# Attention stage: the order of maxima pieces and scores in a step, the causal mask of the maxima, and the sum over experts

## What is computed

```
sx  = einsum('bsh,ndh->bnsd', x, hl_w) + hl_b
q   = einsum('bnsd,neod->bneso', sx, wq);  k = einsum('bnsd,nod->bnso', sx, wk);  v = ...
scores = einsum('bnesd,bntd->bnest', q, k) * d ** 0.5 + causal      # -inf above the diagonal
att = softmax(scores);  qkv = where(pad, 0, einsum('bnest,bntd->bnesd', att, v))
gs  = softmax(einsum('bnsf,nef->bnse', out, gate_w) + gate_b)
mixed = einsum('bnsed,bnse->bnsd', out, gs)                         # the sum over experts
hn  = layernorm(mixed + resid)
```

## Time and profile before

| | us |
|---|---|
| median of 3 runs | 3414.06 (3410.56 to 3416.23) |
| the profiled execution | 3411.35 |
| its span, first to last instruction | 3409.6 |
| PE busy over the span | 3022.5 (89%) |
| DVE busy | 1882.0 (55%) |
| ACT busy | 1284.8 (38%) |
| POOL busy | 1783.4 (52%) |
| line 1899, DVE's reads of maxima, 784 | 859.8 |
| line 1840, exponentials, 776 | 728.5 |
| line 1730, products of the pieces, 1568 | 341.8 |
| line 1735, their mask products, 832 | each 216 to 328 ns long, overlapping |

### The profile page before, as it was taken

One profiled execution on the slowest core, in us unless ns is written; L12 is line 12 of the kernel. 1 busy time (PEld: TensorE's weight loads), 2 busy tenths in 40 slices (PEclk: granted clock), 3 DMA queues, 4 the chain that ended last, 5 costly groups with the idle time before them and its releaser, 6 DMA issues. The chain is left out here.

```text
span 3409.6 us, 46365 instructions
## 1 busy us (share of the span) xinstructions
PE 3022.5 (89%) x18170; PEld 1857.4 (54%) x18170; DVE 1882.0 (55%) x2869; ACT 1284.8 (38%) x1712; POOL 1783.4 (52%) x957
## 2 busy tenths in 40 slices
PE   7998987589998899999999999789899999999953
PEld 3467656378875555555545555455555554545532
DVE  3545764477833456564565641255656465565566
ACT  2232320355533234334434344233343443434433
POOL 0030020332311366777888889546777878888014
PEclk9999888899998899999999999889999999999976
DMA  9961100399960000000000000000000000000001
GB/s 390 423 233 48 55 1 8 112 295 268 267 118 3 1 1 1 1 1 1 1 1 1 1 1 1 1 1 1 1 1 1 1 1 1 1 1 1 1 3 40
DMA packets 63607, 195.24 MB, mean 57 GB/s; under 512 B 8228, under 2 KB 24994, under 8 KB 53411
## 3 DMA queue, kind: packets, MB, share of 16 engines
q1 hardware_dynamic: 38642, 147.98, 11.3%
q0 software_dynamic: 24752, 44.31, 7.2%
HBM read 188.86 MB, written 3.41 MB: 56 GB/s over the span
## 5 line engine op out<-in xcount | busy, mean ns | idle before, releaser
L2029 POOL TENSOR_TENSOR at_acc<-at_acc,at_pt 128x1024 f32<-128x1024 f32 (+3 forms) x674 | 1455.1, 2159 | 271.5 <-ACT at_pt L1840 197.1
L1899 DVE TENSOR_REDUCE at_mx<-at_psR 128x2 f32<-128x1024 f32 (+3 forms) x784 | 859.8, 1112 | 812.4 <-PE at_psR L1730 527.7
L1840 ACT ACTIVATE at_pt<-at_psR 128x1024 f32<-128x1024 f32 (+3 forms) x776 | 728.5, 944 | 971.9 <-PE at_psR L1751 624.3
L1769 PE MATMUL at_psO<-at_pt,v 128*64 128x512 f32 (+3 forms) x3104 | 697.8, 571 | 9.8 <-DVE at_oT L1920 9.8
L1748 PE MATMUL at_psR<-at_qhi,at_klo 64*128 64x512 f32 (+2 forms) x1552 | 344.3, 439 | 68.2 <-DVE at_mx L1899 61.9
L1730 PE MATMUL at_psR<-at_khi,at_qhi 64*128 64x512 f32 (+3 forms) x1568 | 341.8, 430 | 38.8 <-DVE at_mx L1899 9.0
L1769 PEld LDWEIGHTS at_psO<-at_pt,v 128*64 128x64 f32 x3104 | 190.7, 137 | 326.6 <-issue 271.1
L1316 PE MATMUL ga_acc<-h,ga_ring 128*128 128x257 f32 (+1 forms) x1352 | 305.1, 386 | 30.1 <-ACT ga_ring L1210 26.6
L1748 PEld LDWEIGHTS at_psR<-at_qhi,at_klo 64*128 64x128 f32 x1552 | 149.8, 188 | 323.5 <-issue 304.4
L1316 PEld LDWEIGHTS ga_acc<-h,ga_ring 128*128 128x128 f32 (+1 forms) x1352 | 257.9, 193 | 75.6 <-ACT ga_ring L1210 34.7
L1748 PE MATMUL at_psR<-at_qlo,at_khi 64*128 64x512 f32 (+2 forms) x1552 | 298.8, 380 | 0.0
(11 more groups left out here) (331 smaller groups left out, 3442.3 us busy)
## 6 DMA issues: line engine op xcount, KB each, us to landing
gc_rows<-in_adj SPq DMA_DIRECT2D x26, 1664.0 KB, 17.4
ga_rows<-in_adj SPq DMA_DIRECT2D x26, 1664.0 KB, 10.0
ga_ring<-in_adjT POOLq DMA_DIRECT2D x78, 512.0 KB, 23.7
gc_cols<-in_adjT SPq DMA_DIRECT2D x26, 1024.0 KB, 14.9
gc_ring<-in_adjT SPq DMA_DIRECT2D x26, 512.0 KB, 8.0
gc_ring<-in_adjT SPq DMA_DIRECT2D x13, 256.0 KB, 2.8
ga_ring<-in_adjT POOLq DMA_DIRECT2D x13, 256.0 KB, 9.3
out_x<-X SPq DMA_DIRECT2D x6, 512.0 KB
```

The costliest lines, as they stand in the source:

```text
L1769: ins = pe.matmul(columns(psO[lanes[l], :], g), v1[:, t, (2 * hp + l) * D:(2 * hp + l + 1) * D], packed(pt[:, g % PTS, l, 0:w], g), start= ...
L1840: act.activation(pt[:, g % PTS, :, 0:w], psR[:, slot_of["score", g] % SLOTS, :, 0:w], ACT.Exp).then_inc(e_ready, 1)
L1899: dve.tensor_reduce(mx[:, u % 2, :, s, c:c + 1].rearrange("p l o -> p (l o)"), psR[:, slot_of["max", i] % SLOTS, :, 0:w], AX.X, ALU.max).t ...
L2029: pool.tensor_tensor(to, to, got, ALU.add).then_inc(added, 1)
```

## The change

In each step the order score, first piece, score, second piece (and third) becomes first piece, score, score, second piece (and third). The ring's order follows it. The causal mask of the diagonal pieces is no longer added by products: DVE reduces the columns left of the last 128 as before, and the last 128 with a fused add and maximum for each head (`tensor_tensor_reduce`, with `hide_row` now a float mask in SBUF), so a row can have one more partial maximum (`seen`). The four experts are added by one `tensor_reduce` over a view in which the expert is the innermost index, 512 bytes apart, into a new tile; the last block keeps the two additions. The query weights of the second head pair replace the first's in the same buffer by a later load. The core of the diff (declarations of semaphores, and numbers of waits that follow from it, are left out: PE and DVE wait for 8 of `hides` where PE waited for 9):

```diff
@@ slot_users @@
-            for half in range(2):
-                if g + 2 + half < FIRST[NU]:
-                    out.append(("score", g + 2 + half))
-                out += [("max", piece[0]) for piece in max_pieces(u, k, half)]
+            out += [("max", piece[0]) for piece in max_pieces(u, k, 0)]
+            out += [("score", x) for x in (g + 2, g + 3) if x < FIRST[NU]]
+            out += [("max", piece[0]) for piece in max_pieces(u, k, 1)]
@@ AttentionWeights @@
-        self.wq = m.sb("at_wq", [P, NPR, NE, P])
+        self.wq = m.sb("at_wq", [P, NE, P])
-        sp.dma_start(self.wq[:, :, :, :], io["wq2"].rearrange("n p e o -> p n e o")).then_inc(self.loaded, 16)
+        sp.dma_start(self.wq[:, :, :], io["wq2"][0]).then_inc(self.loaded, 16)
@@ stage_attention, tiles @@
-        hide_row = m.sb("at_hide_row", [P, 2, P], BF16)
+        hide_row = m.sb("at_hide_row", [P, P])
+        junk = m.sb("at_junk", [P, P])
-        mx = m.sb("at_mx", [P, 2, 2, SUB, NB + 1])
+        mx = m.sb("at_mx", [P, 2, 2, SUB, NB + 2])
+        mixed = m.sb("at_mixed", [P, SUB, P])
@@ SyncE @@
                 ffn.load(sp, io)
+                for hp in range(1, NPR):
+                    sp.wait_ge(x_full, turn_of["q", FIRST_UNIT[hp] - 1] + 1)
+                    sp.dma_start(wq_sb[:, :, :], io["wq2"][hp]).then_inc(wq_loaded, 16)
@@ TensorE, queries @@
+                    if hp and u == FIRST_UNIT[hp]:
+                        pe.wait_ge(wq_loaded, 16 * hp)
@@ TensorE, row_max @@
-                    diag = c == (c0 // P + s % (bw // P)) // SUB
                     for l in range(2):
                         ins = pe.matmul(psR[:, slot, l, 0:w], qhi[lanes[l], u % 3, s * P:(s + 1) * P],
-                                        khi[lanes[l], kc:kc + w], start=True, stop=not diag)
-                    if diag:
-                        for h in range(2):
-                            for l in range(2):
-                                ins = pe.matmul(psR[:, slot, l, w - P:w], isel[lanes[l], h, :], hide_row[lanes[l], h, :],
-                                                start=False, stop=h == 1)
+                                        khi[lanes[l], kc:kc + w], start=True, stop=True)
                     ins.then_inc(p1_full, 1)
@@ TensorE, main loop @@
-                        for half in range(2):
-                            if g + 2 < ng:
-                                scores(g + 2 + half)
-                            for piece in max_pieces(u, k, half):
-                                row_max(u + 2, *piece)
+                        for piece in max_pieces(u, k, 0):
+                            row_max(u + 2, *piece)
+                        if g + 2 < ng:
+                            scores(g + 2)
+                            scores(g + 3)
+                        for piece in max_pieces(u, k, 1):
+                            row_max(u + 2, *piece)
@@ VectorE, row_max @@
                     dve.wait_ge(p1_full, i + 1)
-                    dve.tensor_reduce(mx[:, u % 2, :, s, c:c + 1].rearrange("p l o -> p (l o)"),
-                                      psR[:, slot_of["max", i] % SLOTS, :, 0:w], AX.X, ALU.max).then_inc(p1_read, 1)
+                    if c < (c0 // P + s % (bw // P)) // SUB:
+                        dve.tensor_reduce(mx[:, u % 2, :, s, c:c + 1].rearrange("p l o -> p (l o)"), got[:, :, 0:w], AX.X,
+                                          ALU.max).then_inc(p1_read, 1)
+                        return
+                    if w > P:
+                        dve.tensor_reduce(mx[:, u % 2, :, s, c:c + 1].rearrange("p l o -> p (l o)"), got[:, :, 0:w - P], AX.X,
+                                          ALU.max)
+                    col = c + (w > P)
+                    if i:
+                        dve.wait_ge(p1_read, i)
+                    link(dve.tensor_tensor_reduce(junk[:, :], got[:, 0, w - P:w], hide_row[:, :], 1.0, -3.0e38, ALU.add,
+                                                  ALU.max, mx[:, u % 2, 0, s, col:col + 1]))
+                    dve.tensor_tensor_reduce(junk[:, :], got[:, 1, w - P:w], hide_row[:, :], 1.0, -3.0e38, ALU.add,
+                                             ALU.max, mx[:, u % 2, 1, s, col:col + 1]).then_inc(p1_read, 1)
@@ VectorE, maxima @@
-                        seen = (c0 // P + s % (bw // P)) // SUB + 1
+                        tile = c0 // P + s % (bw // P)
+                        seen = tile // SUB + 1 + (tile % SUB > 0)
@@ VectorE, gate, piece 2 @@
-                        link(dve.tensor_tensor(on[:, 0:ws, 0:2, :], on[:, 0:ws, 0:2, :], on[:, 0:ws, 2:4, :], ALU.add))
-                        link(dve.tensor_tensor(on[:, 0:ws, 0, :], on[:, 0:ws, 0, :], on[:, 0:ws, 1, :], ALU.add))
+                        if at_block < NPR * NQB - 1:
+                            link(dve.tensor_reduce(mixed[:, 0:ws, :], on[:, 0:ws, :, :].rearrange("p s e c -> p s c e"),
+                                                   AX.X, ALU.add))
+                        else:
+                            link(dve.tensor_tensor(on[:, 0:ws, 0:2, :], on[:, 0:ws, 0:2, :], on[:, 0:ws, 2:4, :], ALU.add))
+                            link(dve.tensor_tensor(mixed[:, 0:ws, :], on[:, 0:ws, 0, :], on[:, 0:ws, 1, :], ALU.add))
-                        dve.tensor_tensor(hsl, hsl, on[:, 0:ws, 0, :], ALU.add).then_inc(mix_done, 1)
+                        dve.tensor_tensor(hsl, hsl, mixed[:, 0:ws, :], ALU.add).then_inc(mix_done, 1)
@@ GpSimd, the mask @@
-                pool.memset(hide_row[:, :, :], 0.0).then_inc(hides, 1)
+                pool.memset(hide_row[:, :], 0.0).then_inc(hides, 1)
+                pool.affine_select(out=hide_row[:, :], in_=hide_row[:, :], compare_op=ALU.is_ge, fill=NEG, base=0,
+                                   pattern=[[-1, P]], channel_multiplier=1).then_inc(hides, 1)
+                pool.wait_ge(hides, 4)
                 for e in range(2):
-                    pool.affine_select(out=hide_row[lanes[e], :, :], in_=hide_row[lanes[e], :, :], compare_op=ALU.is_ge,
-                                       fill=NEG, base=0, pattern=[[D, 2], [-1, P]], channel_multiplier=1).then_inc(hides, 1)
```

More of the change, by code:

```diff
@@ L1450 @@
 UNITS = [(hp, b, e) for hp in range(NPR) for b in range(NQB) for e in range(0, NE, EXPERTS[b])]
+FIRST_UNIT = [[hp for hp, _, _ in UNITS].index(n) for n in range(NPR)]
 LAST_UNIT = {(hp, b): u for u, (hp, b, _) in enumerate(UNITS)}
@@ L1772, in values @@
                     ins.then_inc(pv_done, 1)
-                pe.wait_ge(hides, 9)
+                pe.wait_ge(hides, 8)
                 pe.wait_ge(consts, 3)
@@ L1872, in _ @@
                 dve.wait_ge(zeros, 1)
+                dve.wait_ge(hides, 8)
                 link = Linker(dve, chain)
@@ L1897, in row_max @@
                 def row_max(u, i, s, c, w):
+                    c0, bw = QBLOCKS[UNITS[u][1]]
+                    got = psR[:, slot_of["max", i] % SLOTS, :, :]
                     dve.wait_ge(p1_full, i + 1)
-                    dve.tensor_reduce(mx[:, u % 2, :, s, c:c + 1].rearrange("p l o -> p (l o)"),
-                                      psR[:, slot_of["max", i] % SLOTS, :, 0:w], AX.X, ALU.max).then_inc(p1_read, 1)
+                    if c < (c0 // P + s % (bw // P)) // SUB:
[12 more added lines that the diff above has]
+                                             ALU.max, mx[:, u % 2, 1, s, col:col + 1]).then_inc(p1_read, 1)
                 def maxima(u):
```

4 lines of the change are left out of this document (2 added, 2 removed).

## The result

The changed kernel takes 3363.18 us, median of 4 runs (3360.61 to 3364.28), beside 3412.31 us of the kernel before (3404.88 to 3416.23, 4 runs). The ratio is 0.9857, with a 95% interval from 0.9839 to 0.9876: 49 us faster. Forecast were 7 us, and the low end of the range, 3366 us, was too high by 3.

A forecast was written before the change was run, and what follows sets the result against it. PE was taken to set the pace in its program order, so its waits inside a step count. From 3411.35 us, -6 (order) + 29 - 8 - 4 (mask) - 4 (sum) = 7 gained: 3404 us; likeliest 3392 to 3412, 8 in 10 3366 to 3434.

The forecast's parts named there:

- order, plain two-piece steps: Plain steps with two pieces, 176: the second piece's wait of 0.23 us goes; 40 us gained.
- order, three pieces: Steps with three pieces, 60: the last piece still waits for the first score's exponential, 0.25 us; 5 us lost.
- order, first steps of units: First step of each unit, 48: second piece 0.69 us late behind DVE's work, before 0.23; 22 us lost.
- order, narrow steps: Steps with scores 256 and 128 wide, 44: second piece 0.44 us late in 36, before about 0.2; 9 us lost.
- order, behind gate pieces 0 and 2: Behind gate piece 0 the second piece is 1.3 us late, 10 lost; at gate piece 2 PE stops earlier, 26 lost.
- order, small blocks and unit ends: In small blocks and at unit ends the forecast booked no loss or gain for the order: 0.
- the sum, all gates: At gate piece 2, one reduction of 4.0 us replaces additions of 6.19, so DVE is free 2.2 us sooner; +22.
- the mask: In 208 diagonal pieces PE saves 0.14 us each, 29 gained; DVE's longer reads lose 8 and 4 where not hidden.
- PE's patience is shorter: At gate piece 2, PE gets through less work before stopping than in the old order; with the reduction, 4 us lost.
- rival 4: Products taken off PE stood in waiting time, order worth nothing on balance: 29 shrink to 12, 3421 at worst; chance 0.12.
- rival 3: At gate piece 2 the strided reduction is slower: from 5.7 us it turns the sum over, 7 us gives 3434; chance 0.10.
- Rival 1: New waits for DVE don't come, lateness being absorbed, or the reduction runs at 2.3 us: about 3365; chance 0.19.

The follow-up runs named there:

- The run with half an exponential: The kernel before, order untouched, with ScalarE's exponential over half the columns of each score, leaving out the other half: 3346.84 us, ratio 0.9811.
- near sum: The changed kernel with the reduction reading four neighbouring elements instead of four 512 B apart, leaving out the sum over experts: 3339.46 us, ratio 0.9791.
- mixed order: The changed kernel with the old order at each unit's first and last-but-one step and right behind gate pieces 0 and 2: 3312.73 us, ratio 0.9713.
- GpSimd's halves: The kernel before with GpSimd's running sum in two instructions of 512 elements in place of one of 1024: 3397.61 us, ratio 0.9966.
- near layout: The mixed order with the experts' results laid out so that the four of one sum are neighbours: 3308.96 us, ratio 0.9701.

## Why the prediction was wrong

The sum of the forecast can be cut anew, so that each of its terms has a measured partner: steps of that kind, in the run that has this part alone or, for the mask, added to order and sum. Gains are positive.

| term | forecast | measured |
|---|---|---|
| order, plain two-piece steps | +40 | +51 |
| order, three pieces | -5 | +7 |
| order, first steps of units | -22 | -18 |
| order, narrow steps | -9 | -4 |
| order, behind gate pieces 0 and 2 | -36 | -31 |
| order, small blocks and unit ends | 0 | -11 |
| the sum, all gates | +22 | +34 to +39 |
| the mask | +17 | +12 to +18 |

(The forecast's +40 counts 176 steps, the measured +51 the 148 of them outside the gates' steps. -36 is the -10 behind gate piece 0 and the 26 us by which "PE's patience is shorter" ate the reduction's 2.2 us in ten blocks and 4 more. +17 is 29 - 8 - 4.)

**What each step looks like, right.** The order does trade the wait for ACT against waits for DVE: 26 waits for the reads of maxima became 66 (some 100 were forecast), and they come where they were looked for. The narrow steps wait 0.24 ahead of the second piece, where 0.44 was forecast, and behind gate piece 0 the stall is 1.10 where 1.3 was. At a unit's start the loss has the size but not the place: not the second piece but the first waits, since a piece there waits for DVE's instruction on the queries' low half. The fused instructions cost what the earlier trace rows gave, the reduction 3.8 against 4.0. The mask's net 17 was right in the new order; taken alone it would have been wrong by all of it, since 76 of the pieces' masks stood in the exponential's shadow and DVE's longer reads took back what the others gave. That is rival 4's mechanism, and it holds in the old order only. In the new order, too, there is luck in the 17: by kinds of steps the mask gained 18 to 22 us and lost 6, where 29 and 12 were forecast, and the two misses cancel.

**Failed: the size of a removed wait** ("176 x 0.23 = 40 us gained"). The wait was read off as the gap in PE's starts. The start behind it, 0.43 in the earlier trace rows between piece and values, was taken for a piece's price; 0.10 of it came from the wait. Over the 148 plain steps that are not at gates, 0.345 us each is 51, where 0.23 would be 34; the other 28 of the forecast's 176 stand in the measured row of the gates.

**Failed: the three-piece steps** ("The old stall survives ... 5 lost"). The last piece's wait was seen in the new order, and the old order was given one wait too, for the exponential. The run with half an exponential shows that the old one was for DVE. One stall took the place of another that was longer: 12 us between forecast and run.

**Failed: the length of DVE's absence** ("So DVE is free 2.2 us sooner"). The reduction alone is 2.4 us shorter than the additions that it replaces, about the 2.2 forecast. But 10.76 less 2.2 was taken to leave the 2.71 of the `hn` addition as it stood in the earlier trace rows. That row is no price; the plain price of 512 elements is 0.69, and the rest was waiting for GpSimd. The additions had each been paying it. Absence was 7.22, 1.4 us shorter than forecast, in each large block, 11 us over eight of them. In the old order the clock comes on top, 0.8 us a block on average, which no term had.

The Trainium skill, SBUF — State Buffer, section Who interferes with whom, calls the port pair of VectorE and GpSimd an exclusive lock, in which whoever issues first holds it for the whole instruction. The prediction drew on that section for the reduction, and left out what follows for the addition behind it. The ends at +0.55 agree with it. By its rule the three instructions that read two SBUF operands pay for what is left of a GpSimd instruction, and only one such instruction is left after the change.

The Trainium skill, SBUF — State Buffer, section Door 1: The DMA port swizzle, says that each access that crosses to a new line of 16 bytes pays a penalty, so that by it both strides pay alike. The trace agrees: 0.74 ns an element at 512 bytes and 0.8 at 32, so the upper end of 5.5 us was not needed.

The first two failures are 23 us, the third 11, the smaller losses at gates, narrow steps and first steps some 14; the small blocks, a loss of 11 that no term had, go the other way. That leaves some 5 us of the 42 between 7 and 49 without a name: the parts' sums over steps hold 45 of the 49.

**Two slips in the working**, neither of which moved the forecast. A read of 512 elements costs 0.69 us by the earlier trace rows, not 0.65, so the masked first piece would have been read by 2.17 and not 2.13, still inside 2.18. And rival 3's "from 5.7 us on it turns the sum over" doesn't follow from its own price: at 10 us for each us of the reduction, 7 us gained are used up at 4.7.

**The range.** Rival 1 had the time, about 3365, but not the reason: the losses that it left out did come, and that its number fits is luck. The range's lower end rested on losses absorbed and not on a removed wait being dearer than its gap.

## What to carry to other kernels

Price a removed wait by comparing the same stretch of code with and without it elsewhere in the trace, the restart included, not by the gap alone. Before a part is called worthless, ask what else hides it: the mask's products cost nothing until the wait beside them was gone, so parts that are nothing alone may be worth doing together. A new order need not hold everywhere: kept for plain steps and undone at unit starts, narrow steps and behind gate pieces it gave 99 us instead of 49. And once the longest stall is short, look for the engine that it had hidden: here GpSimd's additions.

## What the runs showed of the hardware

- A `tensor_tensor` on DVE with both operands in SBUF that starts while a GpSimd addition runs ends at a fixed distance behind that addition's end: 0.55 us for 512 elements, 1.08 for 1024, 0.28 for 256, 0.15 for a 128-element product, whatever the GpSimd instruction's length (0.7 to 3.2 us). Of 512, 1024 and 128 elements they take 0.69, 1.22 and 0.29 us alone. Even 32 elements took 1.88 us so (0.19 alone). GpSimd's additions that start while such an instruction runs are longer too, 3.15 and 2.60 us in unit 22 where their mean is 2.39. A `tensor_reduce` of 2048 neighbouring elements took 2.27 to 2.29 us, beside a running addition or not.
- A reduction over fp32 elements 512 bytes apart takes 3.79 us for 2048 elements, over neighbours 2.29. ScalarE's copy of 256 elements takes 384 ns written densely and 642 written 16 bytes apart.
- Behind a wait of some 0.2 us PE needs 0.10 us more until the values' first products than it does in an unbroken row.
- How long PE stood still does not by itself tell its granted clock afterwards. Over the six blocks with gate piece 2: behind 5.84 to 6.18 us (before, changed kernel) it was 1.2 GHz at once in all; behind 3.48 to 3.78 (near sum) at once in four and within a microsecond in two; behind 2.51 to 2.64 (sum alone, mixed order) it was 1.2 GHz within about a microsecond in four of six and stayed at 2.4 in two; behind 1.64 to 1.80 (GpSimd's halves) it fell in two and stayed in four; behind 1.35 to 1.46 (near layout) it stayed at 2.4 in all six. At 1.2 GHz eight value products took 3.6 us instead of 1.94.
